# One gated cross-attention kernel: key masks moved ahead of the last softmax unit, unread matmuls moved and thinned, an offset added as a matmul row

## The reference

```
q = (query @ Wq + bq).reshape(B, Nq, H, D).transpose(0, 2, 1, 3)
k = (key_value @ Wk + bk)...      v = (key_value @ Wv + bv)...
attn = clip(einsum('bhqd,bhkd->bhqk', q, k) * scale, -CLAMP, CLAMP)
attn = softmax(attn, axis=-1)
x = einsum('bhqk,bhkd->bqhd', attn, v).reshape(B, Nq, Cq)
return x @ Wo + bo
x = x + tanh(g_xattn[2]) * (the above)
```

## Time and profile before

| what | us |
|---|---|
| median of three runs | 1306.53 (1298.36 to 1311.1) |
| the profiled execution | 1310.13 |
| its span in the trace | 1308.3 |
| attention of L1 in the span | about 280 to 379 |
| attention of L2 in the span | about 508 to 664 |

### The profile page before, as it was taken

The page is one execution under the profiler, slowest core; times in us unless marked ns, Lnnn a source line. Parts: engine busy times, 40 slices in busy tenths (PEclk is TensorE's granted clock), DMA queues, the critical chain, the costliest instruction groups (busy, mean ns, idle before and its releaser), DMA issues.

```text
span 1308.3 us, 23889 instructions
## 1 busy us (share of the span) xinstructions
PE 901.2 (69%) x8174; PEld 719.9 (55%) x8177; DVE 743.6 (57%) x1872; ACT 489.7 (37%) x1213; POOL 324.2 (25%) x408
## 2 busy tenths in 40 slices
PE   1336261369974765999966699856999998557771
PEld 1224130247764653666645688854777787456671
DVE  5776878755644216667756344446656666532223
ACT  1432154225752341445633332323343433224441
POOL 1000000013413650444400267630000000046661
PEclk9668685569986995767877799987899999779896
DMA  8100000050010117000001011135000000101113
GB/s 210 58 2 1 0 1 0 0 146 1 0 33 19 43 49 213 1 1 0 1 1 33 17 39 42 40 95 140 2 1 0 0 0 1 33 26 41 40 42 109
DMA packets 73150, 48.34 MB, mean 37 GB/s; under 512 B 19642, under 2 KB 65732, under 8 KB 73092
## 3 DMA queue, kind: packets, MB, share of 16 engines
q1 hardware_dynamic: 64484, 31.80, 9.1%
q0 software_dynamic: 6656, 13.64, 3.5%
q10 hardware_dynamic: 1952, 2.15, 0.6%
HBM read 33.93 MB, written 13.63 MB: 36 GB/s over the span
## 4 chain that ended last, share of the span: by engine, by line
PE 46%; DVE 27%; issue 6%; ACT 6%; DMA 6%; another core or an unknown queue 4%; POOL 3%; DVEq 1%; ACTq 0%; SPq 0%; POOLq 0%
PE ps L2049 5%; DMA arena<-rows_x,row_in 4%; PE ps L1850 4%; PE ps L1592 4%; PE ps L2063 3%; PE ps L1912 3%; PE ps L1604 3%; PE ps L1806 2%; PE ps L1870 2%; PE ps L1816 2%; PE ps L1834 2%; PE ps L1895 2%; PE ps L1859 2%; PE ps L1881 2%
## 5 line engine op out<-in xcount | busy, mean ns | idle before, releaser
L534 POOL DMA_INDIRECT arena<-rows_x,row_in x104 | 105.5, 1015 | 224.1 <-DVEq L1204 193.3
L2049 PE MATMUL ps<-arena 128*128 128x128 f32 x1152 | 159.4, 290 | 0.0
L2049 PEld LDWEIGHTS ps<-arena 128*128 128x128 f32 x1152 | 146.7, 203 | 1.7
L2063 PE MATMUL ps<-arena 128*128 x832 | 119.4, 288 | 21.0 <-ACT arena L1541 17.8
L539 POOL DMA_INDIRECT rows_y<-arena,row_out x104 | 107.3, 1032 | 102.8 <-DVE arena L1167 52.5
L2063 PEld LDWEIGHTS ps<-arena 128*128 128x128 f32 x832 | 105.7, 199 | 26.6 <-issue 25.1
L1592 PE MATMUL ps<-q,onesb 128*128 128x256 bf16 x482 | 79.5, 312 | 48.5 <-DVEq L849 48.5
L1154 DVE COPY arena<-arena 128x644 f32 (+1 forms) x104 | 61.0, 587 | 67.6 <-issue 27.2
L1541 ACT ACTIVATE arena<-ps,arena 128x128 f32<-128x128 f32 x256 | 73.4, 375 | 68.0 <-PE ps L2049 56.8
L872 DVE TENSOR_REDUCE arena<-ps 128x8 f32<-128x512 f32 (+1 forms) x96 | 57.2, 596 | 69.4 <-PE ps L1850 63.8
L1604 PE MATMUL ps<-ident,xh 128*128 128x128 f32 x128 | 36.9, 443 | 85.9 <-DVE xh L595 70.1
(11 more groups left out here) (295 smaller groups left out, 1806.2 us busy)
## 6 DMA issues: line engine op xcount, KB each, us to landing
arena<-rows_y SPq DMA_DIRECT2D x20, 256.0 KB, 4.8
arena<-in_L_ffn_w SPq DMA_DIRECT2D x2, 2048.0 KB, 9.2
arena<-in_L_ffn_w SPq DMA_DIRECT2D x16, 256.0 KB, 6.5
rows_x<-xh SPq DMA_DIRECT2D x3, 1024.0 KB, 5.1
rows_x<-zero SPq DMA_DIRECT2D x1, 2560.0 KB, 10.2
arena<-in_L_ffn_gate_proj SPq DMA_DIRECT2D x8, 256.0 KB, 5.2
arena<-in_L_ffn_up_proj SPq DMA_DIRECT2D x8, 256.0 KB, 5.1
arena<-in_L_ffn_down_proj SPq DMA_DIRECT2D x1, 2048.0 KB, 9.9
```

The costliest lines, as they stand in the source:

```text
L534: g.indirect_dma_start(xq[:, q % 4, :], None, rows_x, bass.IndirectOffsetOnAxis(row_in[:, q:q + 1], 0)).then_inc(sem(f"xq_loaded{q % 4}"), 16)
L2049: ins = pe.matmul(ps[:, 2 * m + s_ % 2, P * f:P * f + P], wst[:, s_ % 4, lo:lo + P], xqT[:, s_ % 2, :], start=True, stop=True)
L2063: ins = pe.matmul(ps[:, 4 + s_ % 2, 0:P], hT[:, s_ % 2, f, :], w2[:, P * f:P * f + P], start=(f == 0), stop=(f == NF - 1))
```

## The change

On VectorE, `keys(i + 1)` moves ahead of `scores(i, 3)` in both L1 and L2, and the addition of the offset to all of x goes; instead one row of the offset (1 x 128, not yet scaled by the gate) is copied out of PSUM. On TensorE, L2's output projection gets one more accumulating matmul for each half group, of a row of ones by the offset row, so that the gate is applied with the rest in line 937. The unread matmuls ahead of a turn go from three to one in L1 and to two in L2; those behind the queries and keys go from eight to four in L1 and stay eight in L2 (24 in group 0 stay). In L2 ten new ones follow the value rows of each group but the last. Layer L3's attention keeps its program and its form of the offset.

```
--- before.py
+++ after.py
@@ -190,6 +190,7 @@
         bv2 = sb("bv2", [P, 1])
         bvs = sb("bvs", [P, P])
         offset = sb("offset", [P, P])
+        offset_row = sb("offset_row", [1, P])
         lng = sb("lng", [P, 8])
 
         gw = {1: sb("gw1", [P, E]), 2: sb("gw2", [P, E]), 3: sb("gw3", [P, E])}
@@ -960,17 +961,15 @@
                             inverse(i - 1, 3)
                         scores(i, 1)
                         inverse(i, 0)
-                        if first and l == 2:
-                            add_offset()
                         if older:
                             add_group(i - 2)
                         scores(i, 2)
                         inverse(i, 1)
                         if older:
                             group_statistics(i - 2)
-                        scores(i, 3)
                         if more:
                             keys(i + 1)
+                        scores(i, 3)
                         inverse(i, 2)
                         return
                     else:
@@ -1006,7 +1005,10 @@
                     v.tensor_copy(bvs[:, :], bv2[:, 0:1].to_broadcast([P, P])).then_inc(sem("bvs_ready"), 1)
                 if l > 1:
                     v.wait_ge(sem("offset_mm"), l - 1)
-                    own(v.tensor_scalar(offset[:, :], ps[:, 4, 0:P], gates[:, l:l + 1], None, ALU.mult), "offset_ready")
+                    if l == 2:
+                        own(v.tensor_copy(offset_row[:, :], ps[0:1, 4, 0:P]), "offset_ready")
+                    else:
+                        own(v.tensor_scalar(offset[:, :], ps[:, 4, 0:P], gates[:, l:l + 1], None, ALU.mult), "offset_ready")
                 keys(0)
                 if l == 3:
                     scores(0, 0)
@@ -1864,7 +1866,7 @@
                 def turn(i, u):
 
                     if l != 3:
-                        dense(2 + u % 2, 3)
+                        dense(2 + u % 2, l)
                     pe.wait_ge(sem("prob"), UNITS * i + (UB[l] + u + 1))
                     for k in range(sub):
                         ins = pe.transpose(ps[:, 2 + u % 2, P * k:P * k + P], t["p"][:, u, P * k:P * k + P], ident[:, :])
@@ -1909,7 +1911,9 @@
                         for k in range(n):
                             lt = t["o"][:, P * hh:P * hh + P] if l != 3 else \
                                 t["o"].rearrange("p (k n) -> p k n", k=8)[:, k, P * hh:P * hh + P]
-                            ins = pe.matmul(o, lt, wo[l][:, k, :], start=(k == 0), stop=(k == n - 1))
+                            ins = pe.matmul(o, lt, wo[l][:, k, :], start=(k == 0), stop=(k == n - 1 and l != 2))
+                        if l == 2:
+                            ins = pe.matmul(o, ones[:, :], offset_row[:, :], start=False, stop=True)
                     ins.then_inc(sem("att_mm"), 1)
 
                 def group(i, first=False, more=True):
@@ -1928,11 +1932,13 @@
                         scores(i, 3)
                         if more:
                             queries_keys(i + 1)
-                        dense(2, 24 if first else 8)
+                        dense(2, 24 if first else 4 * l)
                         turn(i, 0)
                         if not first:
                             values(i - 1, 3)
                         value_rows(i)
+                        if l == 2 and more:
+                            dense(3, 10)
                         return
                     value_rows(i)
                     scores(i, 2)
```

## The result

| | before | changed |
|---|---|---|
| median, us | 1305.22 (1298.36 to 1311.1, 4 runs) | 1321.76 (1313.73 to 1322.64, 4 runs) |
| ratio | | 1.0154, 95% from 1.0099 to 1.0209 |
| profiled execution | 1310.13 | 1322.64 |
| L1, first scores to last projection | 94.5 | 101.0 |
| L2, first scores to last projection | 148.9 | 154.0 |

The kernel became 1.5% slower; I had predicted 1299, faster by 0.6%. The two profiled executions differ by 12.5 us: 6.5 in L1, 5.1 in L2, 1.3 ahead of L1, -0.3 between the two, nothing behind. Both attentions lost, and L2 was to gain 12.4.

A forecast was written before the change was run, and what follows sets the result against it. TensorE was taken to bound both attentions, in L2 through its clock. L2's -12.4 us and L1's +4.7 gave -7.7: 1302.4 from the profiled 1310.1, 1299 for the median, with an 8 in 10 range of 1280 to 1320.

The forecast's parts named there:

- Keys first: In L2, key masks end at 601.9, two us sooner, so TensorE's wait of 2.02 us all but goes.
- Ten unread matmuls: In L2, ten take 1.1 us, one fewer in each of four turns returns 0.4: +0.7 us of TensorE a group.
- The row: Two one-row matmuls added to each L2 group's projection: 0.6 us for the pair, between 0 and 0.9.
- The period at the full clock: An L2 group takes 15.2 us, between TensorE's own 14.5 and 16.1 for the chain by the value copy.
- The number of falls: In L2 the clock falls once, 0 to 3 possible, each costing 7.2 us: +7.2.
- The ends of L2: Group 0 gives -0.8 us; group 7 starts warm for -1.0, and the row in the last two projections adds +0.6.
- L1: Period 9.3 us, wait before the projection about 0.95, two groups of 14.1 us at the lower clock: +4.7 us.
- The first: Rival: L1 keeps its clock and gives -4.9 us, 1289 in all, or 1282 with no L2 fall; chance 0.27.
- The second: Rival: L1 loses its clock for most of its loop; 1313 with five slow groups, 1323 with seven; chance 0.18.
- The third: Rival: in L2 new waits replace the old, the clock falls every other group, L2 gives about 0; 1311, chance 0.15.

The follow-up runs named there:

- a: The changed kernel with L1's unread matmuls put back, keys still first in both layers; 1323.85 us, ratio 1.0111 to the kernel before.
- b: The kernel before with only L1's unread matmuls thinned to one and four; 1304.38 us, ratio 0.9926.
- e: a with the value copy issued ahead of unit 3's exponential in L2 only; 1295.62 us, ratio 0.9865 to the kernel before.
- the five kernels with all three edits: e, f, g, k and l: in L2 value copy first, keys first and ten unread matmuls behind the value rows; L2 124.8 to 126.4 us.
- d: a with the offset added to all of x by VectorE as before, without the row matmuls; 1305.24 us, ratio 0.9979 to the kernel before.
- c: The kernel before with only the key masks moved ahead of unit 3's softmax, in L2 alone; 1314.74 us, ratio 1.0039.
- f: d with the value copy issued ahead of unit 3's exponential in L2; 1291.43 us, ratio 0.9843 to the kernel before.
- j: The kernel before with, in L2 alone, key masks ahead of unit 3's softmax and value copy ahead of its exponential; 1296.29 us, ratio 0.9974.
- g: f with L1's unread matmuls thinned and the old order of the keys in L1; 1287.56 us, ratio 0.9822 to the kernel before.
- h: g with four unread matmuls behind L2's value rows instead of ten; 1287.19 us, ratio 0.9811 to the kernel before.
- k: g with the value copy first in L1 too; 1272.23 us, ratio 0.9759 to the kernel before.
- l: The changed kernel with the value copy ahead of unit 3's exponential in L1 and L2; 1277.55 us, ratio 0.9798 to the kernel before.

## Why the prediction was wrong

**Keys first: right as far as it went.** The wait for the masks goes (no idle at 588.59). The masks themselves take 1.53 us (586.53 to 588.06) where I had 1.1 from the earlier trace rows.

**Ten unread matmuls: right.** 1.19 us (587.40 to 588.59) against 1.1.

**The row: under-priced.** I took 0.6 us for the pair, between 0 and 0.9. Projection and row now take 556.36 - 554.73 = 1.63 us at full clock against 0.61 in the earlier trace rows: 1.02 us, above my upper end. The two row matmuls themselves take 0.41 us each, 0.82 in all, inside my bounds; but the projection's own two, which took 0.61 side by side, take 0.39 and 0.42 between them. That slowing of the neighbours was not in my sum. These are the rows, of the timeline of TensorE in the changed kernel:

```profile
554.73 0.46 PE L1914 MATMUL ps<-wo,arena 128*128 128x128 f32 x2 [1.38 <-ACT arena L1439]
555.12 0.48 PE L1916 MATMUL ps<-offset_row,ones 1*128 1x128 f32 x2
555.53 0.49 PE L1914 MATMUL ps<-wo,arena 128*128 128x128 f32 x2
555.95 0.48 PE L1916 MATMUL ps<-offset_row,ones 1*128 1x128 f32 x2
556.36 0.69 PE L1883 MATMUL ps<-arena 128*64 128x64 f32 x16
```

**The period at the full clock: the chain was right, the choice was not.** I worked out 14.5 us for TensorE alone and 16.1 for the chain by the value copy, and took the middle, 15.2, with a wait of 0.7 us. Both bounds are in the trace, in turn: the group behind a fallen one runs at TensorE's 14.58 us, since the other engines have caught up during the slow group, and in the next one the chain's wait appears almost whole, 1.37 us of the 1.6 that lie between the two (14.58 + 1.37 = 15.95 against 16.1). A middle value describes neither group.

**The number of falls: this is the step that failed.** "I reckon with one (0 to 3 possible): +7.2." It was three, one behind each appearance of that wait. The slow groups took 22.5, 25.5 and 24.0 us instead of 22.4, because the row and the ten unread matmuls are slow in them too. Six groups with three falls: 652.62 - 538.40 = 114.2 us, where 91.2 + 3 x 7.2 = 112.8 by my own terms. That these agree so well is partly luck: the three groups at full clock took 42.3 us (group 1, which has no projection, only 13.1) instead of 45.6, and the three slow ones 72.0 instead of 67.2. The gain of 11.2 us over these groups became a loss of 4.6. The ends of L2 add the rest: -0.5 in group 0 (I had -0.8) and +1.0 behind the first scores of group 7, where I had -0.4.

**L1: right in mechanism and nearly in size.** Period 9.24 us against 9.3, wait 0.93 against 0.95, two groups at the lower clock (13.2 and 14.0 us against 14.1), +6.5 us against +4.7; the fall in the last group, at 370.1, is in the difference. I had given the cause to fewer unread matmuls and longer wait together, and a and b show that it takes both.

**The rivals.** The first, that L1 keeps its clock, fell. The second needed five groups or more at the lower clock, and there were two. The third is what happened: "the new wait for the value copy (behind the later softmax of unit 3) and the offset row [...] take its place, and the clock still falls every other group." It gave 0 for L2 and 1311 in all; L2 lost 5.1 us, L1 1.8 more than I had, and the total is 1322. I held the twenty-two unread matmuls ahead of that wait against it. e shows that they don't outweigh it: they are the same there, and it is the wait that is gone. By the rule of the Trainium skill that I set aside (TensorE: Matmul & The Clock Gate, section "Why this matters for your kernels"), waits this short would leave the clock alone; the changed kernel speaks against it once more, down to a wait of 0.91 us in L1 (313.65), behind which the clock fell at 315.4.

**What stays open.** Why the stretch behind L2 varies between 638.4 and 656.0 us with the same code was not tried. It is as large as the whole effect of the change, and I had told it only as a spread of the runs. Why one wait of a given length costs the clock and the next does not is open too. And since each kernel has one trace, how much its number of falls differs from execution to execution is not shown; what speaks against chance is that the five kernels with all three edits have none in L2.

## What to carry to other kernels

When a late result is moved ahead in an in-order queue, follow what it pushes back through the next engine's queue to the instruction that stands behind it there: here a copy that needed nothing of the delayed softmax stood behind an exponential that did, and one swap of the two turned a loss of 1.5% into a gain of 2.0%. Where a wait costs the clock, its price is not its length but a whole group at the lower clock, so the sum should take the upper value of that wait in steady state and ask in how many groups it appears, not average it away. Here filler matmuls helped most once no wait was left that they could not reach: ten of them (with one fewer ahead of each turn) gave little before the swap (L2 143.8 against 147.7, d and c), more behind it (125.5 against 136.9, f and j) and, with ten instead of four behind it, L2 went from 131.0 to 126.3 and kept its clock.

## What the runs showed of the hardware

- A matmul with an input of one row cost as much as the one with 128 beside it: at full clock the row of 1x128 took 0.41 us (555.12 to 555.53), the projection's matmul of 128x128 beside it 0.42 (555.53 to 555.95). The Trainium skill (TensorE: Matmul & The Clock Gate, section "Why this matters for your kernels") says in its row on small contractions that a single matmul with 32 input rows takes the time of one with 128; the trace agrees and goes down to one row. It also shows that the mix has a price: the projection's two matmuls of 128 input rows took 0.61 us back to back and 0.81 us with a row matmul behind each.
- In L1 the clock was lost with a recurring wait of about 0.93 us in a group of 9.2 (behind the first and the last of its four occurrences at full clock), and kept with 0.57 us in a group of 8.9. At the place where the last waits stand in L1, it was lost behind 1.64 to 1.66 us (b, g, h) and kept behind 1.20 us (k, l) and 1.05 us (before). In L2 it was kept with 0.73 us in every group of 14.7 (f). With 1.38 us (h) it held behind the wait at 582.26 and fell at 598.6 behind the next: not each such wait costs the clock.
- The price of the same instructions was 11 us or none: a matmul row of 1 us a group cost 11.3 us of L2 where the clock was already falling (a against d), and nothing where TensorE had a gap of 0.73 us for it (e against f).
